# Routing and expert stage of a graph and mixture-of-experts block joined in one program block

## The reference

```python
x = x + gnn(layernorm(x), edge_index, ...)          # second layer: one head, 768 wide
xf = layernorm(x)
gw = softmax over the best 2 of 4 groups            # xf @ Wg + bg
ew = softmax over the best 4 of 8 experts, by group # xf @ We + be
for each expert e:                                  # 768 -> 384 -> 768
    o = gelu(xf @ W1[e] + b1[e]) @ W2[e] + b2[e]
    y = y + o * gw[group of e] * ew[e]
x = x + y
```

## Time and profile before

| what | us |
| --- | --- |
| median of 3 runs (lowest, highest) | 1514.7 (1512.83, 1516.56) |
| the profiled execution | 1514.43 |
| its span, first to last instruction | 1512.0 |
| around the span | 2.43 |
| PE, DVE, ACT, POOL busy | 1359.7, 1158.2, 742.5, 505.5 |
| mean granted TensorE clock | 0.971 of full |

### The profile page before, as it was taken

How to read it: one execution, slowest core, us unless ns; L and a number is a source line. 1 busy time by engine, 2 the same in 40 slices (tenths; PEclk the granted TensorE clock), 3 DMA queues, 4 the chain that set the end, 5 groups by cost and what they waited for, 6 DMA issues and landing times. The chain is left out here.

```text
span 1512.0 us, 31335 instructions
## 1 busy us (share of the span) xinstructions
PE 1359.7 (90%) x7728; PEld 1132.7 (75%) x7739; DVE 1158.2 (77%) x1823; ACT 742.5 (49%) x1171; POOL 505.5 (33%) x557
## 2 busy tenths in 40 slices
PE   6898999787787789899968999999999999999995
PEld 4665666533233358799957999999999999999995
DVE  6499999799999978768877566555565755887882
ACT  3565665345655544412225455444454545665661
POOL 1000000003334300122324555555455555555563
PEclk9999999699999999999969999999999999999998
DMA  6300020232221242234578878767778876889953
GB/s 234 139 18 17 10 80 18 78 124 87 69 74 61 68 120 86 75 86 108 124 211 240 231 204 213 174 165 172 167 199 207 214 179 162 220 266 276 256 121 47
DMA packets 102255, 211.68 MB, mean 140 GB/s; under 512 B 19318, under 2 KB 58486, under 8 KB 102082
## 3 DMA queue, kind: packets, MB, share of 16 engines
q1 hardware_dynamic: 79186, 142.06, 28.7%
q0 software_dynamic: 22240, 66.69, 21.7%
q10 hardware_dynamic: 784, 2.36, 0.4%
HBM read 164.14 MB, written 54.93 MB: 145 GB/s over the span
## 5 line engine op out<-in xcount | busy, mean ns | idle before, releaser
L1004 PE MATMUL ps_o<-prob,h_head 128*97 128x512 f32 (+1 forms) x480 | 188.1, 529 | 51.5 <-DVE prob L946 51.5
L2082 POOL DMA_INDIRECT out_nodes<-y,to_index x92 | 158.7, 1725 | 138.5 <-issue 88.3
L2399 PE MATMUL ps_h<-e_hi,e_xt_hi 128*128 (+1 forms) x546 | 191.2, 350 | 7.7 <-ACT e_xt_hi L2201 4.4
L2384 PE MATMUL ps_y<-e_hi,e_ht_hi 128*128 (+1 forms) x546 | 192.3, 352 | 6.0 <-issue 3.2
L1004 PEld LDWEIGHTS ps_o<-prob,h_head 128*97 128x97 f32 x480 | 73.4, 165 | 165.6 <-issue 89.9
L2384 PE MATMUL ps_y<-e_lo,e_ht_hi 128*128 (+1 forms) x546 | 184.3, 337 | 0.0
L2384 PE MATMUL ps_y<-e_hi,e_ht_lo 128*128 (+1 forms) x546 | 184.2, 337 | 0.0
L2399 PE MATMUL ps_h<-e_lo,e_xt_hi 128*128 (+1 forms) x546 | 183.6, 336 | 0.0
L2266 DVE TENSOR_TENSOR e_lo<-raw,e_hi (+1 forms) x189 | 175.8, 952 | 7.3 <-ACT e_hi L2209 6.6
L2219 ACT ACTIVATE y<-ps_y,gate 128x768 f32 (+1 forms) x91 | 82.1, 902 | 189.0 <-PE ps_y L2384 103.9
L838 ACT ACTIVATE score<-score,al_col 128x1250 f32<-128x1250 f32 x80 | 106.0, 1334 | 98.8 <-DVE score L889 98.8
(11 more groups left out here) (357 smaller groups left out, 3046.3 us busy)
## 6 DMA issues: line engine op xcount, KB each, us to landing
raw<-in_ew SPq DMA_DIRECT2D x192, 384.0 KB, 5.5
w_room<-rel_dram SPq DMA_DIRECT2D x14, 640.0 KB, 4.5
b_all<-in_eb SPq DMA_DIRECT2D x32, 192.0 KB, 6.0
al_src<-al_dram SPq DMA_DIRECT2D x1, 5000.0 KB, 14.7
xs<-in_x SPq DMA_DIRECT2D x5, 768.0 KB, 12.5
x_in_t<-in_x SPq DMA_DIRECT2D x10, 384.0 KB, 3.5
out_nodes<-x SPq DMA_DIRECT2D x10, 384.0 KB, 4.1
table<-xf SPq DMA_DIRECT2D x10, 384.0 KB, 2.6
```

The lines of the kernel that those rows point to most:

```text
L1004: turn = nc.tensor.matmul(ps_o[u][0:C1 + 1, c, 0:WID[c]], h_head[:, u, t, :], prob[:, t % 2, 512 * c:512 * c + WID[c]], start=(t == 0), st ...
L2082: nc.gpsimd.indirect_dma_start(out, bass.IndirectOffsetOnAxis(to_index[:, w:w + 1], 0), y[:, w, :], None, bounds_check=NP - 1, oob_is_err= ...
L2384: last = nc.tensor.matmul(ps_y[:, half, 0:HALF], a, b[:, bass.ds(u, 1), at:at + HALF].rearrange("p o d -> p (o d)"), start=(m == 0), stop= ...
L2399: nc.tensor.matmul(ps_h[:, 0:HID], xt_hi[:, c, :], b[:, bass.ds(e % 2, 1), c * HID:(c + 1) * HID] .rearrange("p o m -> p (o m)"), start=(c ...
```

## The change

All five engines' routing parts become functions (`route_sync` and so on) that `run_experts` calls at the head of its own block, so there is no end of a block between the two. The PSUM tensors are shared (`ps_first`, `ps_h_2`, `ps_mix1`, `ps_xf`, `ps_gates`), the expert buffers are placed by hand where they don't overlap what the routing still reads, and gathers alternate between two semaphores. In the routing part now stand: the low parts of W1 (three) and of W2 (three) of expert 0, on POOL; the high parts of W2 of expert 0 on ACT; four gathers straight from the list instead of two from a copied index; the rows, transposes, splits and the first product of tile 0; `match` and sum of list 3; the load of b1. SP loads expert 1's weights after gather 0 has landed. A Gelu of one column loads ACT's table early. The 8 and 18 empty transposes are gone, 12 stand earlier. The two last `add_bias` of POOL come after gather 3 and the copy of the gates of tile 2; `ready`, for which ACT waits ahead of the first Gelu, is set there too.

```diff
-        with nc.Block() as block:
-            @block.sync
-            def _(sp):
...
+        def route_sync(sp):
...
+            load_bias(sp, s, b1, 0)
...
+            sp.wait_ge(gates_out, 16 * NT)
+            sp.wait_ge(s.gathered, 16)
+            for piece in range(3):
+                sp.wait_ge(s.w1_in[piece], 16)
+                load_first(sp, s, w1, 1, piece)
...
+            load_bias(sp, s, b1, 1)
+            sp.wait_ge(s.gathered, 32)
...
+            for piece in range(3):
+                pool.wait_ge(w1_hi_made, piece + 1)
+                at = piece * PIECE
+                nc.gpsimd.tensor_tensor(s.e1_lo[:, 0, at:at + PIECE], s.raw1[:, 0, at:at + PIECE],
+                                        s.e1_hi[:, 0, at:at + PIECE].bitcast(F32),
+                                        ALU.subtract).then_inc(w1_lo_ready, 1)
+            add_bias(NT - 3, bias_added[(NT - 3) % 2])
...
+            rest_of_second(0)
+            rest_of_second(1)
+            pool.wait_ge(gates_out, 16 * NT)
+            pool.wait_ge(filled, 5)
+            pool.wait_ge(list_kept, 1)
+            gather(0, s.gathered)
+            rest_of_second(2)
+            pool.wait_ge(list_kept, 2)
+            gather(1, s.gathered_1)
+            pool.wait_ge(s.gathered, 16)
+            keep_gates(0)
+            pool.wait_ge(list_kept, 3)
+            pool.wait_ge(s.rows_kept, 1)
+            pool.wait_ge(s.gate_kept, 1)
+            gather(2, s.gathered)
+            pool.wait_ge(s.gathered_1, 16)
+            keep_gates(1)
+            pool.wait_ge(list_kept, 4)
+            pool.wait_ge(s.rows_kept, 2)
+            pool.wait_ge(s.gate_kept, 2)
+            gather(3, s.gathered_1)
+            pool.wait_ge(s.gathered, 32)
+            keep_gates(2)
...
+            exp(NT - 1)
+            for piece in range(3):
+                act.wait_ge(s.w2_in[piece], 16)
+                at = piece * PIECE
+                nc.scalar.activation(s.e2_hi[:, 0, at:at + PIECE], s.raw2[:, 0, at:at + PIECE],
+                                     ACT.Copy).then_inc(w2_hi_ready, 1)
+            split_gates(NT - 2)
+            nc.scalar.activation(gelu_row[:, :], half_neg[:, :], ACT.Gelu)
+            keep_bias(NT - 2)
+            split_gates(NT - 1)
+            act.wait_ge(s.x_turned, 1)
...
+            turn_nothing(nc, s, ps_l[:, 0:P], 12)
+            list_now(1)
...
+            weigh_bias(NT - 2)
+            turn_gates(NT - 1)
+            turn_x(0)
+            list_now(2)
+            first_product()
+            list_now(3)
+            turn_x(1)
+            weigh_bias(NT - 1)
+
+        run_experts(nc, s, w1, b1, w2, out, (route_sync, route_gpsimd, route_scalar, route_vector, route_tensor))
...
+                route_gpsimd(pool)
...
                 pool.sem_inc(ready, 1)
...
+                for u in range(2):
+                    pool.wait_ge(s.bias_kept, NT - 1 + u)
+                    add_bias(NT - 2 + u, scattered[u])
+                nc.gpsimd.memset(y[:, 0, :], 0.0).then_inc(first_set, 1)
...
+                tile(0, first=True)
+                with pool.Fori(0, pool.snap(pairs)):
                     tile(1)
+                    tile(0)
...
+                def second_tile(k, e):
+
+                    weights(1, 0, (0,))
+                    add_bias(k, e)
+                    weights(1, 0, (1, 2))
+                    keep(0)
+                    split_x(2)
+                    keep_rows(3)
+                    match(AHEAD, 3, rows_made)
+                    weights(1, 1, (0, 1))
+                    rest_of_h(1)
+                    weights(1, 1, (2,))
```

More of the change, by code:

```diff
@@ L3 @@
 from contextlib import ExitStack
+import math
 F32 = mybir.dt.float32
@@ L2004, in expert @@
                 tiles = tiles_of(eng, e)
-                if alone and not last:
+                if start:
+                    with eng.If(tiles > 1):
+                        one(e, 1, early=True)
+                    with eng.If(tiles < 2):
+                        first_alone()
+                    with eng.If(tiles > 2):
+                        with eng.Fori(2, tiles):
+                            one(e, 2)
+                elif alone and not last:
                     with eng.If(tiles > 1):
@@ L2221, in keep_y, with first_tile, tile @@
                                          .rearrange("p o c -> p (o c)")).then_inc(y_made, 1)
-                def tile(k, e, which, start, last):
+                def first_tile():
+                    act.wait_ge(biased, 1)
+                    nc.scalar.activation(h_act[:, :], h_in[:, :], ACT.Gelu).then_inc(gelued, 1)
+                    split_x(1)
+                    act.wait_ge(h_turned, 1)
+                    nc.scalar.activation(ht_hi[:, :, :].rearrange("p k n -> p (k n)"), ps_t[:, 0:HID],
+                                         ACT.Copy).then_inc(h_hi_made, 1)
+                    weights(1, 0)
+                    weights(1, 1)
+                def tile(k, e, which, start, last, early):
+                    if start:
+                        first_tile()
+                        return
                     head = which == 0
                     if head and not last:
-                        if not start:
-                            act.wait_ge(h_summed, k)
+                        act.wait_ge(h_summed, k)
                         weights(e + 1, 0)
@@ L2287, in first_tile, with first_alone, tile @@
                                             ALU.subtract).then_inc(h_lo_made, 1)
+                def first_tile():
+                    dve.wait_ge(b1_in, 16)
+                    add_bias(0, 0)
+                    start = dve.value_load(s.starts[0:1, AHEAD - 2:AHEAD - 1], min_val=LEAD, max_val=LIST - NT)
+                    dve.wait_ge(s.route_listed, AHEAD - 1)
+                    mark_padding(nc, s, ps_l).then_inc(matched, 1)
+                    dve.wait_ge(matched, 1)
+                    keep_list(nc, s, ps_l, start).then_inc(s.route_kept, 1)
+                    split_x(1)
+                    rest_of_h(0)
+                    keep_rows(2)
+                    dve.wait_ge(s.route_kept, AHEAD - 1)
+                    match(AHEAD - 1, 2, rows_made)
+                def second_tile(k, e):
[9 more added lines that the diff above has]
+                    weights(1, 1, (2,))
+                def first_alone():
                     weights(1, 0, range(3))
+                    keep(0)
                     match(AHEAD, 3, rows_made)
-                def tile(k, e, which, start, last):
+                    weights(1, 1, range(3))
+                def tile(k, e, which, start, last, early):
                     if start:
                         first_tile()
+                        return
+                    if early:
+                        second_tile(k, e)
                         return
```

1131 lines of the change are left out of this document (573 added, 558 removed).

## The result

The changed kernel takes 1525.7 us (median of 4 runs, 1524.23 to 1528.37), the kernel before, run beside it, 1513.76 (4 runs, 1512.78 to 1516.56). The ratio is 1.0076, 95% interval 1.0057 to 1.0096: slower by some 0.8%, clear of noise.

The account below looks back on a forecast made before the run. PE was taken to bound the kernel, so only when tiles 0, 1 and 2 get through it counts. Delays up to tile 2 of +12.2 less 1.2 regained gave +11.0 on 1514.43: 1525.4 us, range 1510 to 1531.

Parts of the forecast that it names:

- the sign: Whole kernel: slower, given 0.69, against same 0.17 and faster 0.14.
- C: List 0 to product 0: 11.9 us in place of 16.6, leaving product 0 +3.5 in all.
- F: After the low part of h, up to product 7: a third of 3.7 us of stalls is taken back, -1.2.
- rival 1: Routing to first products: POOL and DVE don't hold each other, bias rows land before the scatter; 1507.9 us, chance 0.14.
- A: Ninth ranking: POOL's three W1 low parts hold DVE, making it 5.0 us late.
- B: Tenth ranking: POOL's first two W2 low parts hold DVE, +3.2 us, list 0 at 793.4.
- the upper end: Price of a POOL subtraction beside DVE: 1.83 us of hold each, rather than the lower end of 0.95.
- D: Product 0 to product 1: 10.0 us against 7.3, +2.7, with low clock and a new wait for ready.
- E: Up to tile 2: later bias adds delay the scatter of tile 0 (+10.5); low part of h up to +12.2.
- rival 4: Tile 1: clock stays 0.50 for another product and down, 3 us on top; 1528.5 us, chance 0.10.
- Rival 3: DVE is held, but bias rows are covered, so the train follows product 1; 1519.5 us, chance 0.19.
- rival 2: No hold of DVE, but the bias rows are late; 1516.5 us, chance 0.17.

Follow-up runs that it names:

- w1_on_dve: Changed kernel with the three low parts of W1 of expert 0 moved from POOL to DVE; 1520.23 us, 1.0049 of the kernel before.
- w2_on_dve: Changed kernel with the three low parts of W2 of expert 0 moved from POOL to DVE; 1521.59 us, 1.0057 of the kernel before.
- w2_behind_loads: w2_behind, with SP issuing expert 1's weights when gather 1, not gather 0, has landed; 1511.44 us, 0.9981 of the kernel before.
- w2_behind: bias_ahead with DVE's three low parts of W2 put behind h_in of tile 0 and list 3; 1510.93 us, 0.9976 of the kernel before.
- narrow_bias: Changed kernel with the last two additions of weighted b2 carrying 16 columns instead of 768 (computes less); 1521.78 us.
- both_on_dve: Changed kernel with the low parts of both W1 and W2 of expert 0 moved from POOL to DVE; 1517.17 us, 1.0021 of the kernel before.
- bias_ahead: both_on_dve with the last two bias adds ahead of gathers 2 and 3, and ready set earlier; 1511.49 us, 0.9975 of the kernel before.
- bias_only: Changed kernel with only the order of bias_ahead, low parts staying on POOL; 1521.22 us, 1.0046 of the kernel before.

## Why the prediction was right, point by point

The time was forecast as 1525.4 and measured as 1525.7; the sign, and both mechanisms that carry the sum (POOL's subtractions hold DVE, and the bias adds come too late), are shown by the runs. That the two times agree to 0.3 us is luck. Steps C to F were each off by one or two us, the forecast was +11.0, and the change is +11.9 in the medians and +13.3 at the last product in the trace.

- **The reading of the stretch.** I misread the row 770 to 772 of the earlier trace rows: 0.79 is PE, 1.39 is DVE, ACT has none and POOL has 1.80. DVE was not nearly idle there, so that point for rival 1 falls. No term of the sum hangs on it.
- **A** (+5.0): 5.86, L1738 held under all three. The 0.5 that I let slip through was wrong: POOL began 0.1 us into L1738, so nothing slipped. **B** (+3.2): 1.63 + 0.96 = 2.6; here a reduction, with one operand in SBUF, took its usual 0.48 at 787.73 while POOL was at the second subtraction, and with the steps to and from it more than my 0.5 went by. Sum 8.4 at list 0, forecast 8.2. The choice of the upper end is borne out: 6.06 covers three whole subtractions (5.88) and 1.96 one, and the 1.15 of the earlier trace rows was the rest of an addition. The Trainium skill, page "SBUF — State Buffer", section "SBUF: two separate sides", has the port pair locked for the whole instruction; the trace agrees, with 6.06 us beside 5.88. w1_on_dve and w2_on_dve show that the subtractions, and not their place in the code, are the cause.
- **C** (list 0 to product 0, 11.9): 12.9. The third subtraction, with the issue of gather 0 ahead of it, cost 2.4 in place of 1.8. Product 0 was +4.6, not +3.5.
- **D** (10.0 from product 0 to product 1): 10.4, right in size, the cause mistaken. The Gelu began at 816.69, before POOL's copy of the gates (817.36), with no idle time of ACT ahead of it, so `ready` did not hold it. It was `h_in` behind the copy of the rows of tile 1 and a match (0.9 after the product), and the Gelu behind ACT's copy of bias rows. The half clock was right: 5.65 for product 0, forecast 5.2. The wait for gather 1 was put at nothing, because "DMA is idle for most of this stretch". The two shares of the earlier trace rows are not typical even of before, where the share is 1.01 to 1.06 from 784 to 790 and 1.04 on average from 808 to 830. With the change gather 1 took 8.3 us from the start of its issue to its landing, and ahead of the weights (w2_behind_loads) it has landed at least 2.8 us earlier than behind them (w2_behind).
- **E** (scatter +10.5): +12.4. `h_in` of tile 0 was +6.3 for the reasons in C and D, forecast +3.9 (its terms add up to 3.8); the second issue came 5.1 behind it, forecast 6.1; from issue to scatter 10.9, forecast 10.3. But POOL's wait was 3.63, not the 6 or more that was to show it, since 4.5 of the 10.9 are its own preparation, and narrow_bias gives back 2.9 of the 12.4, not most of it: what made the scatter late was chiefly that `h_in` and the issues ahead of it were late. The low part of `h` in this step was at +14.1, forecast +12.2. I called it and the `down` behind it those of tile 2; they are of tile 1, in the step of tile 2.
- **F** (-1.2): here the sum has what I missed. After PE's wait of 3.9 us for the rows of tile 3 the clock was 0.50 (0.87 from 832 to 834, 0.50 from 834 to 842), and the 18 matmuls of the `down` took 5.9 us (0.32 each) in place of 3.1 (0.17 each): product 3 is +15.8. I had the low clock only at product 0 and, as rival 4, at tile 1. And then 3.2 us were regained by product 7, not 1.2. Left: +12.6, and +0.7 to the last product. The medians moved by 11.9.
- **The rivals.** Rival 1 had product 0 at 6.5 earlier without holds: both_on_dve shows 6.2. Its other half, that the bias rows land in time, is false; together with them (bias_ahead) it is 1511.5, where rival 1 said 1507.9. Rival 3 is narrow_bias or bias_only, 1521.8 and 1521.2, where it said 1519.5; rival 2 is both_on_dve, 1517.2, where it said 1516.5. Rival 4 is false where it stood, as the clock was 1.00 from 814 to 832; its low `down` came a step later, and is in F.

Against the kernel before, then: holds +8.4; the shorter way to the first product -3.8 (at product 0 +4.6); `h_in`, Gelu and clock up to product 1 +3.1; bias rows, the match and low part put ahead, and clock, up to product 3 +8.1; regained -3.2. The last two are net 4.9; bias_only gives back 4.8, which is the same size, though it does not show that it is the same time.

## What to carry to other kernels

A subtraction moved to an idle GpSimd is not free when VectorE runs a chain of short instructions with two operands in SBUF beside it: here six of 1.8 us put the first product back by 10.8 us, where the same work on VectorE, mostly in its own waits, cost nothing up to there. When a stage is pulled forward, list what is queued behind each accumulating DMA on its engine and issue those first; here two bias adds in the wrong place cost 5 us whether the stage was early or late. And a stall can be paid twice on TensorE: here once for a wait of 3.9 us and once for the 2.8 us that the next 18 matmuls took longer at the half clock.
